# Bias of the layer-1 heads added by TensorE as two one-row products; layer-2 fp8 rows normalised and scaled by ScalarE

## The reference, cut to what matters

```python
# layer 1, cross attention (x is layer-normalised first, cond is the context)
q = (x @ Wq + bq).reshape(1, B * N, H, hd)
kv = (cond @ Wkv + bkv).reshape(1, -1, 2, H, hd)
q = jnp.transpose(q * scale, (0, 2, 1, 3))
q = _fq_sym(q, axis=-1)      # s = max(max|x| / 127, 1e-8); q = clip(round(x / s), -127, 127) * s
k = _fq_sym(k, axis=-1)
...
# layer 2, feed-forward, on layer-normalised rows
scale_x = jnp.maximum(jnp.max(jnp.abs(x2d)) / 448.0, 1e-06)
x8 = (x2d / scale_x).astype(jnp.float8_e4m3fn)
```

## Time and profile before

| what | us |
|---|---|
| median of 3 runs (lowest, highest) | 3404.22 (3401.59, 3406.93) |
| the profiled execution, its own time | 3412.33 |
| its span in the trace | 3410.3 |
| TensorE busy | 2727.4 (80%) |
| VectorE busy | 2490.0 (73%) |
| ScalarE busy | 1909.4 (56%) |
| GpSimd busy | 602.4 (18%) |

### The profile page before, as it was taken

How to read it: one execution, slowest core, us unless ns; L and a number is a source line. 1 busy time by engine, 2 the same in 40 slices (tenths; PEclk the granted TensorE clock), 3 DMA queues, 4 the chain that set the end, 5 groups by cost and what they waited for, 6 DMA issues and landing times. The chain is left out here.

```text
span 3410.3 us, 63176 instructions
## 1 busy us (share of the span) xinstructions
PE 2727.4 (80%) x21404; PEld 1416.1 (42%) x21404; DVE 2490.0 (73%) x4757; ACT 1909.4 (56%) x2773; POOL 602.4 (18%) x539
## 2 busy tenths in 40 slices
PE   5768999686799999999996677686789628859983
PEld 3344444333465656565663433333211213334542
DVE  5746677656799999999994666624499796676548
ACT  2554433232599999999992533321578332844541
POOL 4341000012110101010104233303021610020013
PEclk8978999897899999999998888887899859978996
DMA  4433420200000000000000200010332010032301
GB/s 149 170 140 115 155 75 37 90 0 16 19 13 7 13 7 13 7 13 7 7 0 16 87 0 0 18 59 13 75 75 50 22 50 0 1 85 50 67 8 53
DMA packets 65341, 152.00 MB, mean 45 GB/s; under 512 B 11841, under 2 KB 20049, under 8 KB 63377
## 3 DMA queue, kind: packets, MB, share of 16 engines
q1 hardware_dynamic: 62368, 140.43, 13.8%
q0 software_dynamic: 2800, 9.18, 0.8%
HBM read 93.61 MB, written 24.38 MB: 35 GB/s over the span
## 5 line engine op out<-in xcount | busy, mean ns | idle before, releaser
L1617 DVE TENSOR_REDUCE s_top<-ps 128x1 f32<-128x512 f32 x1024 | 657.3, 684 | 30.4 <-PE ps L1512 29.9
L1586 ACT ACTIVATE s_prob<-ps,s_shift,m_sq 128x1024 int16<-128x1024 f32 x512 | 615.1, 1202 | 30.6 <-DVE s_shift L1625 30.6
L1512 PE MATMUL ps<-s_ks,s_qs 128*128 128x512 f16 x1024 | 352.5, 386 | 61.0 <-issue 14.8
L1517 PEld LDWEIGHTS ps<-ident,s_prob 128*128 128x128 f16 x4096 | 272.7, 98 | 123.5 <-DVE m_o L1635 51.5
L1517 PE MATMUL ps<-ident,s_prob 128*128 128x128 f16 x4096 | 314.2, 220 | 0.7 <-ACT s_prob L1586 0.5
L1505 PE MATMUL ps<-s_ks,s_qs 128*128 128x512 f16 x1024 | 307.5, 382 | 1.0 <-ACT s_prob L1586 0.5
L1592 ACT ACTIVATE s_probT<-ps 128x1024 f16<-128x1024 int16 x256 | 262.2, 1024 | 7.0 <-PE ps L1517 6.6
L1008 PE MATMUL ps<-m_hT,m_w 128*128 128x512 f16 x1024 | 232.3, 381 | 1.8 <-PEq L105 1.8
L249 PE MATMUL ps<-ident,s_parts 128*128 128x128 f16 x640 | 77.4, 296 | 129.2 <-POOL s_parts L240 127.5
L1630 DVE CAST s_probT<-ps 128x1024 f16<-128x1024 int16 x256 | 174.4, 681 | 4.7 <-PE ps L1517 4.7
L2289 DVE TENSOR_SCALAR s_prob<-ps,s_cap 128x1024 f32<-128x1024 f32 x128 | 158.2, 1270 | 25.8 <-PE ps L2198 25.8
(11 more groups left out here) (403 smaller groups left out, 5708.5 us busy)
## 6 DMA issues: line engine op xcount, KB each, us to landing
s_qs<-m_qT SPq DMA_DIRECT2D x144, 128.0 KB
s_ks<-m_kT SPq DMA_DIRECT2D x96, 128.0 KB
numbers<-s_numbers SPq DMA_DIRECT2D x21, 512.0 KB, 2.7
s_slabs<-numbers SPq DMA_DIRECT2D x21, 512.0 KB, 5.9
m_ks<-context_parts SPq DMA_DIRECT2D x12, 512.0 KB
expert_rows<-s_y SPq DMA_DIRECT2D x19, 256.0 KB, 2.0
s_rows_in<-in_ctx SPq DMA_DIRECT2D x16, 256.0 KB
x_sb<-in_L_ffn_W_up SPq DMA_DIRECT2D x4, 1024.0 KB, 6.0
```

Source lines behind the costliest of these rows:

```text
L1512: pe.matmul(quarter_at(q), qs[:, hb, bass.ds(t * P, P)], ks[:, hb, cols(q, 512)], start=True, stop=True).then_inc(s.top_scored, 1)
L1517: j = pe.transpose(turned(half, F16)[:, cols(m, P)], prob[:, u, cols(8 * half + m, P)].bitcast(F16), k.ident[:])
L1586: act.activation(prob[:, u, cols(half, HALF)], pair(half).rearrange("p m n -> p (m n)"), ACT.Exp, bias=shift[:, u:u + 1], scale=sq[:, bass ...
L1617: dve.tensor_reduce(top4[:, u, q:q + 1], quarter_at(q), AX.X, ALU.max).then_inc(s.top_read, 1)
```

## The change

In `quantised_heads` the bias comes as one row (`bias_row`). ScalarE casts it to float16, VectorE subtracts the cast from it, and these two parts are multiplied by a row of ones (set by GpSimd): two products with one row of weights (`ones`) and 512 columns, that follow the 12 products of each tile and add the bias in PSUM. TensorE waits for both parts before the first tile. VectorE reads the maximum and the scaling straight from PSUM; the scaling of the queries and the multiplication by `scale` are one instruction. The bank is given back after the scaling (`scaled_ready`), and the wait for GpSimd (`rows_used`) stands right ahead of the write to `rows`.

In `fp8_rows` VectorE makes only offsets (-mean x rstd, four small instructions). ScalarE normalises all 16 tiles into `normal`, VectorE takes the maxima, and ScalarE scales the stored tiles into `rows`, which has two groups now. ScalarE's copies of the weights come in two halves behind the normalising and behind the first eight scalings, and TensorE's turns of the weights in two halves around the product for the maximum. The loops are written out.

```diff
...
     L = 1 if parts is None else 2
...
-        bias_bc = s.sb("bias_bc", [P, D], F32)
+        bias_row = s.sb("bias_row", [1, D], F32)
+        bias_parts = s.sb("bias_parts", [1, 2, D], F16)
+        ones = s.sb("ones", [1, P], F16)
...
         @s.block.sync
         def _(sp):
-            sp.dma_start(bias_bc[:], bias.partition_broadcast(P)).then_inc(s.bias_loaded, 16)
+            sp.dma_start(bias_row[:], bias.unsqueeze(0)).then_inc(s.bias_loaded, 16)
 
         @s.block.tensor
         def _(pe):
             pe.nop().then_inc(s.turned, 1)
             def project(t, u):
-                pe.wait_ge(s.biased, max(t - 1, 0) if isinstance(t, int) else t - 1)
+                pe.wait_ge(s.scaled_ready, max(t - 1, 0) if isinstance(t, int) else t - 1)
                 for m, (lx, lw) in enumerate(PARTS):
                     for c in range(DC):
                         i = pe.matmul(k.ps[:, u, :], src[:, lx, c, bass.ds(t * P, P)], w[:, lw, c, :],
-                                      start=(m == c == 0), stop=(m == 2 and c == DC - 1))
+                                      start=(m == c == 0), stop=False)
+                for l in range(2):
+                    i = pe.matmul(k.ps[:, u, :], ones[:], bias_parts[:, l, :], start=False, stop=(l == 1))
                 i.then_inc(s.projected, 1)
 
...
                 pe.wait_ge(k.context_first, 16 * k.context_loads)
+            pe.wait_ge(s.ones_ready, 1)
+            pe.wait_ge(s.bias_lo, 1)
             project(0, 0)
...
         @s.block.vector
         def _(dve):
             v = Steps(dve, s.vsteps)
-            dve.wait_ge(s.bias_loaded, 16)
-            with v.loop(T // 2, 10) as i:
+            dve.wait_ge(s.bias_hi, 1)
+            dve.tensor_tensor(bias_parts[:, 1, :], bias_row[:], bias_parts[:, 0, :], ALU.subtract).then_inc(s.bias_lo, 1)
+            with v.loop(T // 2, 4 + 2 * L) as i:
                 for u in range(2):
                     t = 2 * i + u
                     dve.wait_ge(s.projected, t + 1)
-                    if L == 2:
-                        dve.wait_ge(s.rows_used, t + 1)
-                    dve.tensor_tensor(rows[:, u, :], k.ps[:, u, :], bias_bc[:], ALU.add).then_inc(s.biased, 1)
-                    dve.wait_ge(s.biased, t + 1)
-                    v.done(dve.tensor_reduce(amax[:], rows[:, u, :].rearrange("p (h d) -> p h d", d=HD), AX.X,
+                    v.done(dve.tensor_reduce(amax[:], k.ps[:, u, :].rearrange("p (h d) -> p h d", d=HD), AX.X,
                                              ALU.max, apply_absolute_value=True))
                     v.done(dve.tensor_scalar(step[:, u, :], amax[:], scale / 127.0, 1e-8, ALU.mult, ALU.max))
...
                     v.done(dve.reciprocal(inv[:], step[:, u, :]))
-                    if scale != 1.0:
-                        v.done(dve.tensor_scalar(inv[:], inv[:], scale, None, ALU.mult))
-                    v.done(dve.tensor_tensor(scaled[:, u, :].rearrange("p (h d) -> p h d", d=HD),
-                                             rows[:, u, :].rearrange("p (h d) -> p h d", d=HD),
-                                             inv[:].unsqueeze(2).broadcast_to([P, H, HD]), ALU.mult))
+                    dve.scalar_tensor_tensor(scaled[:, u, :].rearrange("p (h d) -> p h d", d=HD),
+                                             k.ps[:, u, :].rearrange("p (h d) -> p h d", d=HD), scale,
+                                             inv[:].unsqueeze(2).broadcast_to([P, H, HD]), ALU.mult, ALU.mult
+                                             ).then_inc(s.scaled_ready, 1)
+                    dve.wait_ge(s.scaled_ready, t + 1)
                     if L == 1:
                         dve.wait_ge(s.turned, 2 * i + 1)
                         dve.tensor_scalar(f16[:, u, 0, :], scaled[:, u, :], ROUND, ROUND, ALU.add,
@@ -1304,14 +1307,16 @@
                     else:
                         v.done(dve.tensor_scalar(scaled[:, u, :], scaled[:, u, :], ROUND, ROUND, ALU.add,
                                                  ALU.subtract))
+                        dve.wait_ge(s.rows_used, t + 1)
                         dve.tensor_tensor(rows[:, u, :].rearrange("p (h d) -> p h d", d=HD),
                                           scaled[:, u, :].rearrange("p (h d) -> p h d", d=HD),
                                           step[:, u, :].unsqueeze(2).broadcast_to([P, H, HD]),
                                           ALU.mult).then_inc(s.rows_ready, 1)
 
-        if L == 2:
-            @s.block.gpsimd
-            def _(pool):
+        @s.block.gpsimd
+        def _(pool):
+            pool.memset(ones[:], 1.0).then_inc(s.ones_ready, 1)
+            if L == 2:
                 pool.nop().then_inc(s.rows_used, 2)
                 with pool.Fori(0, T // 2) as i:
                     for u in range(2):
...
         @s.block.scalar
         def _(act):
             out = ints if parts is None else parts
+
+            act.wait_ge(s.bias_loaded, 16)
+            act.activation(bias_parts[:, 0, :], bias_row[:], ACT.Copy).then_inc(s.bias_hi, 1)
 
             def hi(t, u):
                 if L == 2:
...
 def fp8_rows(k, out, scale, weights):
...
         layernorm_buffers(k, s)
-        rows = s.sb("rows", [P, R, D], F32)
+        normal = s.sb("normal", [P, T, D], F32)
+        offset = s.sb("offset", [P, T], F32)
+        rows = s.sb("rows", [P, 2, R, D], F32)
...
         def _(dve):
-            for t in range(0, T, R):
-                dve.wait_ge(s.rstd_ready, t // R + 2)
-                for u in range(R):
-                    v.later(dve.tensor_scalar(rows[:, u, :], k.x[:, t + u, :], k.mv[:, t + u, 0:1],
-                                              k.rstd[:, t + u:t + u + 1], ALU.subtract, ALU.mult))
-                v.catch_up()
-                v.done(dve.tensor_reduce(amax[:, t:t + R], rows[:], AX.X, ALU.max, apply_absolute_value=True))
+            for i in range(T // R):
+                group = cols(i, R)
+                dve.wait_ge(s.rstd_ready, i + 2)
+                dve.scalar_tensor_tensor(offset[:, group], k.mv[:, group, 0], -1.0, k.rstd[:, group], ALU.mult, ALU.mult
+                                         ).then_inc(s.offset_ready, 1)
+            for i in range(T // R):
+                dve.wait_ge(s.normal_ready, R * (i + 1))
+                v.later(dve.tensor_reduce(amax[:, cols(i, R)], normal[:, cols(i, R), :], AX.X, ALU.max,
+                                          apply_absolute_value=True))
+            v.catch_up()
             dve.tensor_reduce(top[:], amax[:], AX.X, ALU.max).then_inc(s.max_ready, 1)
             dve.wait_ge(s.max_ready, 1)
             dve.tensor_copy(wide_top[:], top[:].broadcast_to([P, P])).then_inc(s.spread, 1)
             dve.wait_ge(s.total_ready, 1)
             v.done(dve.tensor_reduce(total[:], k.ps[:, 3, 0:P], AX.X, ALU.max))
             v.done(dve.tensor_scalar(scale, total[:], 1.0 / 448.0, 1e-6, ALU.mult, ALU.max))
-            v.done(dve.reciprocal(inv[:], scale))
-            v.done(dve.tensor_scalar(fac[:], k.rstd[:], inv[:, 0:1], None, ALU.mult))
-            with v.loop(T // R, R + 3) as i:
-                for u in range(R):
-                    t = R * i + u
-                    v.later(dve.tensor_scalar(rows[:, u, :], k.x[:, t, :], k.mv[:, t, 0:1],
-                                              fac[:, bass.ds(t, 1)], ALU.subtract, ALU.mult))
-                v.catch_up()
-                fp8_round(v, dve, rows[:].rearrange("p r d -> p (r d)"), bits[:].rearrange("p r d -> p (r d)"))
+            dve.reciprocal(inv[:], scale).then_inc(s.inv_ready, 1)
+            for i in range(T // R):
+                dve.wait_ge(s.scaled, R * (i + 1))
+                fp8_round(v, dve, rows[:, i % 2, :, :].rearrange("p r d -> p (r d)"), bits[:].rearrange("p r d -> p (r d)"))
                 dve.wait_ge(s.turned, R * i + 1)
                 for u in range(R):
-                    dve.tensor_tensor(numbers[:, u, :], rows[:, u, :], bits[:, u, :], ALU.subtract
+                    dve.tensor_tensor(numbers[:, u, :], rows[:, i % 2, u, :], bits[:, u, :], ALU.subtract
                                       ).then_inc(s.numbers_ready, 1)
                 dve.wait_ge(s.numbers_ready, R * i + R)
 
         @s.block.tensor
         def _(pe):
...
-            turn_weights(k, s, pe, weights, slabs, weight_banks(weights, 0, 1))
+            turn_weights(k, s, pe, weights, slabs, weight_banks(weights, 0, 2))
             pe.wait_ge(s.spread, 1)
             pe.matmul(k.ps[:, 3, 0:P], wide_top[:], k.ident32[:], start=True, stop=True).then_inc(s.total_ready, 1)
-            with pe.Fori(0, T // R) as i:
-                for u in range(R):
-                    pe.wait_ge(s.numbers_ready, R * i + u + 1)
-                    pe.wait_ge(s.copied, R * i + u + 1)
-                    for c in range(DC):
-                        j = pe.transpose(k.ps16[:, u, cols(c, P)], numbers[:, u, cols(c, P)], k.ident[:])
-                    j.then_inc(s.turned, 1)
```

(55 more changed lines are left out.)

## The result

The changed kernel takes 3395.95 us (median of 9 runs, 3391.58 to 3401.46); the kernel before took 3403.30 beside it (9 runs). The ratio is 0.9976, with a 95% interval of 0.9967 to 0.9986: 8.2 us less by the ratio, between 4.8 and 11.2 (the two medians differ by 7.35). The forecast was -12.4 and 3391.8. The direction is right and the time lies in the range; a third of the forecast gain is missing. Of all executions behind this document one, of `e_quarter`, took 3541.22 us at a mean granted clock of 0.79 instead of 0.90, and is left out of its numbers.

A forecast was written before the change was run, and what follows sets the result against it. VectorE was taken to pace the keys, with the queries' leader left open. Keys -5.1, queries -0.1 and fp8 rows -7.2 summed to -12.4 us, from 3404.2 to 3391.8, range 3386 to 3402.

The forecast's parts named there:

- TensorE becomes the bound of the keys: Keys' steady part: VectorE needs 3.05 us a tile after the change, TensorE 3.49, so TensorE sets the pace.
- Its pace, 3.49: Keys: TensorE's tile takes 0.47 us for the turn plus 14 products of 0.216, 3.49 instead of 4.13.
- The term for 14 products: Keys and queries: 12 products and two one-row ones a tile, each at 0.216 us, taken from a 98-row product.
- the second rival: Keys and queries: one-row products don't overlap, 0.46 us each, 14.7 more in 30 gaps; total +2.3, 3406.5; chance 0.08.
- 3.26, the gain only 0.2 a tile: Queries: TensorE's half turn (0.24 us) and 14 products set 3.26 a tile instead of 3.48; 15 gaps gain 3.7.
- The starts: Keys and queries: TensorE waits for the bias before its first product; 5.8 us lost in keys, 4.2 in queries.
- The first rival: Keys: VectorE's step keeps meeting GpSimd, tiles stay 4.13 to 4.15 us, 10.6 more; total -1.8, 3402.4; chance 0.12.
- I expect a mixture whose mean is TensorE's: Keys, against the first rival: TensorE gets ahead after a late tile, so the next escapes GpSimd; mean pace stays TensorE's 3.49.
- the tail: Keys: the last tile's own chain loses the bias addition, a gain of 0.7 us.
- Scaling from PSUM: Keys and queries, VectorE: the three-input scaling from PSUM takes 0.75 us where a tensor-tensor instruction takes 0.69, +0.06.
- fp8 rows: The fp8 stage: ScalarE normalises and scales, VectorE's groups take 7.4 us instead of 9.89; -7.2 us in all.
- cover of the third group: fp8 rows: ScalarE's copies and scalings end at 2789.7, VectorE wants group 3 at 2789.8; missing it costs up to 0.5.

The follow-up runs named there:

- e_quarter: Against the changed kernel, only four of sixteen fp8 weight copies stand ahead of the scale, eight behind the first scalings, four later; 3393.21 us, ratio 0.9967.

## Why the prediction was right or wrong, step by step

- **TensorE becomes the bound of the keys: right.** Busy 54.64 of 55.00 us. **Its pace, 3.49: wrong.** The step that failed is "I take 0.216, since a product of 98 rows, with one of 128 behind it, has the next start 0.22 later". The row was real, and the value for a product too (0.215 with four). But 98 rows lie on the side of 128, and one row does not, so the row held no change of the kind that the one-row pair has twice a tile. ("No row has fewer" is true of the rows shown. The trace before has products of 96 rows at L2779, and one of 16 rows at L366, alone and with 16 columns; they don't price such a change either.) The term for 14 products wanted 0.21 more: 3.1 us in the keys (54.26 against 51.13) and 3.2 in the queries (52.10 against 48.87). The prediction had a bound for it (0.46 each, the second rival), and the truth, 0.43 + 0.21 = 0.64 for the pair or 0.32 each, lay between the ends. It isn't quite that rival's mechanism: a load is exposed, but once at each change of rows and not at each one-row product, since two more of them cost 0.215 each.
- **Queries: "3.26, the gain only 0.2 a tile": wrong for the same reason.** 0.21 dearer a tile eats the 0.2, and the 15 gaps are as before (52.10, 52.17).
- **The starts: right in kind, too dear.** Keys +5.1 for 5.8, queries +2.5 for 4.2. The row of 2 KB landed and was taken up 2.9 us after its issue (4.6 forecast) in the keys, and 1.32 us after it in the queries, where I had taken the 2.50 of the earlier trace rows. That row is a load of another shape, to 128 partitions. So TensorE started 1.7 and 1.25 us earlier than forecast. The first tile then took 6.03 us in the keys for the forecast 5.0, since the clock stayed at 0.50, and 4.89 for 5.3 in the queries. Together the starts gave back 2.4 us; the share of it that hangs on when the clock rose is luck of the one execution.
- **The first rival (step meets GpSimd): its mechanism is there, its verdict isn't.** "I expect a mixture whose mean is TensorE's" is what the long steps show at three paces: 9, 6 and 3 of 16 where the gaps are 3.62, 3.41 and 3.19 us on average (one-row pair, 128-row pair, one product). With four products, at 4.05 us, it is 5, and most of the others are a little longer too (up to 0.37 us). The last tile's step lasted 1.13, which is why the tail gained 0.1 and not 0.7.
- **Scaling from PSUM: 0.69, not 0.75** (one of after: 655.23 to 655.92), VectorE's own tile 3.01 for the forecast 3.05.
- **fp8 rows: right in the sum and in its parts.** Normalising 11.39 (11.5), copies 7.36 (7.5), groups 7.38 (7.4), cover of the third group kept, ScalarE and not the scale last. From the normalising's start to the first scaling it took 18.5 us (19.0 forecast), which is the 0.4 that came on top.

The sum came out 3.9 us too good: the gaps 2.9 and 3.6 (nearly all of it, 6.4, is the change of rows), plus 0.1 from the tails, less 0.7 and 1.7 from the starts and 0.4 from the fp8 rows; the last tenth is rounding.

So the direction and the place in the range were earned by the fp8 rows alone. The heads were forecast at -5.2 and came out at -0.9 by their stages, and their own measurement shows no change (ratio 1.0001).

## What to carry to other kernels

A row of the trace prices only what it contains: before using the nearest one, ask what the new instruction does differently from its neighbours, and not only how large it is. Put a wait where its data are used and not ahead of the whole stage, above all on the engine that leads. When adding a rank-one term on TensorE, fill the operand up to the neighbours' number of rows (here 96 were enough) and put all parts into one product. Before reading a start out of one profile, look at the granted clock in it.

## What the runs showed of the hardware

- A pair of products of 1, 32 or 64 rows among products of 128 rows costs 0.21 us a visit more than one of 96, 98 or 128; the products' number doesn't matter (0.215 us each with two and four of one row, and with one and two of 128). In the profile the load unit is idle for 0.42 us ("issue") at each change, and the load starts with its product instead of 0.2 us ahead of it.
- A DMA of 2 KB to one partition was taken up 1.3 to 1.6 us after its issue in the queries, where the queue was empty, and 2.9 to 3.6 us after it in the keys, behind the 4 MB of the context.
- Behind about 26 us of TensorE idle the granted clock of its first 5 us was 0.50 in one execution and 0.73 in another, with the same first 12 products; from its first product to VectorE's first tile it took 4.5 to 6.1 us in eight profiles.
- When VectorE's small step can meet GpSimd's 1.15 us and another engine sets the pace, the lag appears as longer steps; the list of waits showed 2.3 us where VectorE had 9.1 us to spare.
